# Weight conversions issued without a wait on the conversion before, in a layer of FFT attention and ternary feed-forward on eight cores

## The chip, the cores and the metric

The kernel runs on the 8 cores of one Trainium2 chip. Each core takes one of the 8 batch entries and computes it whole; the cores exchange nothing. The time is the device time of the slowest core, in microseconds (us).

## The reference

For each batch entry `x` is 2048 x 1024 (tokens x features), f32:

```python
xn = layernorm(x)                                 # over the 1024 features
q, k, v = xn @ Wq.T, xn @ Wk.T, xn @ Wv.T         # 1024 x 1024 each
mem = cumsum(fft(k) * fft(v), over the tokens)
attn = real(ifft(mem * conj(fft(q))))
h = silu(xn @ w1.T * w1_s) * (xn @ w2.T * w2_s)   # 4096 wide, weights -1, 0 or 1
h = gelu(h @ h1.T * h1_s)                         # 4096 x 4096
h = gelu(h @ h2.T * h2_s)                         # 4096 x 4096
return x + attn + h @ w3.T * w3_s
```

## The kernel before, in words

Activations lie with the features on the partitions and the tokens along the free dimension. Every f32 operand of a matrix product is split into a bf16 high part and a bf16 rest, and the products that matter are summed in PSUM; the ternary weights are exact in bf16.

There is no scheduler that reorders. `S.op(engine, emit, reads, writes, ...)` appends an operation to one list; each engine later executes its own operations in the order of that list. A tracker for each buffer holds the token of its last write and of the reads since. An operation waits for the last write of all that it reads, and for the last write and the reads of all that it writes. A DMA counts a semaphore up by 16 when it has landed; with `dma_sem` a name of its own is given to that semaphore. Loads are issued by SyncE (SP), stores to DRAM and the conversions below by GpSimd (POOL). A wait holds up everything behind it on its engine's list.

The stages:

1. Constants, the first layernorm (`emit_ln(0)`: x tile loaded to `XT`, sums by TensorE on L316 and L325, result `XNH` and `XNL`, stored to `xnh_scr` and `xnl_scr` by POOL on L368 and L371). Then Wq, Wk, Wv are multiplied with the Fourier matrices (L424) and written to DRAM as `wl_k`, `wl_v`, `wl_q`. A fence follows: every engine's next operation waits for all of this.
2. Conversion of the feed-forward weights from f32 to bf16, DRAM to DRAM, by DMAs on POOL's queue (L448 to L457): `w1c` to `w1b`, `w2c` to `w2b`, `h1c` to `h1b`, `h2c` to `h2b`, `w3c` to `w3b`. Each DMA reads 4 MB and writes 2 MB; there are 4 + 4 + 16 + 16 + 4 = 44. They write different parts of their tensor, but the tracker knows only the tensor as a whole, with one semaphore for each of the five.
3. Attention, 8 tiles of 256 tokens (`NT_A`, L459 on). In each: 24 projections (`proj`, L463: 8 each for k, v, q). One projection loads a slab `SLA` (L466, 512 KB, three buffers in turn; a slab's rows are runs of 512 bytes) on SP's queue, does 24 matmuls (L476) and a copy by ScalarE (L485). VectorE does the products and the scan over tokens. Then come the layernorm of the next tile (`emit_ln(t + 1)`) and the inverse transform: for each of 8 output chunks 32 matmuls (L570) into one of four PSUM banks, an add of x by VectorE into `ptc0` or `ptc1` in turn (L586), and a store to `part_scr` by POOL (L589). On POOL's list the 44 conversions stand first, then the `xnh_scr` and `xnl_scr` stores of tile 1, then the `part_scr` stores of tile 0, and so on.
4. A second fence, and the feed-forward: 4 tiles of 512 tokens (L593 on). L620 multiplies with w1 and w2, L657 with h1 and h2, L687 with w3; weights come from `w1b` to `w3b` by SP. The results go to `y`.

Of the kernel before, what the change touches and what calls it, by code (L numbers as in the profile page):

```python
# [58 lines left out]
class _Sched:  # L59
# [17 lines left out]
        return [(s, v, None, True) for s, v in self.counts.items() if v > 0]  # L77

    def op(self, eng, emit, reads=(), writes=(), extra_waits=(), dma=False,
           dma_sem=None):  # L80
        waits = {}
        def _add(tok):
            if tok is None:
                return
            sem, val, peng, pdma = tok
            if waits.get(sem, (0,))[0] < val:
                waits[sem] = (val,)
        for b in reads:
            _add(b.w)
        for b in writes:  # L90
            for t in b.rs:
                _add(t)
            _add(b.w)
        for t in extra_waits:
            _add(t)
        for t in self.fence_pending.pop(eng, ()):
            _add(t)
        if dma_sem is not None:
            sem = dma_sem
            amt = 16  # L100
            self.counts.setdefault(sem, 0)
        elif dma:
            i = self.rr[eng]
            self.rr[eng] = (i + 1) % self.NDMA
            sem = {"sync": "ds", "gpsimd": "dg", "scalar": "dc"}[eng] + str(i)
            amt = 16
            if self.counts[sem] > 0:
                _add((sem, self.counts[sem], None, True))
        else:
            sem = {"tensor": "tns", "vector": "vec", "scalar": "act"}[eng]  # L110
            amt = 1
        self.counts[sem] += amt
        tok = (sem, self.counts[sem], eng, dma)
        self.ops.append((eng, emit, [(s, v[0]) for s, v in waits.items()], sem, amt))
        for b in reads:
            b.rs.append(tok)
        for b in writes:
            b.w = tok
            b.rs = []
        return tok  # L120
# [22 lines left out]
def build_nc():  # L143
# [144 lines left out]
    def T(obj, tag=None):  # L288
        key = (id(obj), tag)
        if key not in trk:  # L290
            trk[key] = _Trk()
        return trk[key]
# [10 lines left out]
    for dst, src in ((s1c, s1m), (s2c, s2m), (sh1c, sh1m), (sh2c, sh2m), (s3c, s3m)):  # L303
        S.op("sync", lambda h, d=dst, s=src: h.dma_start(out=d[:], in_=s),
             writes=[T(dst)], dma=True)
# [97 lines left out]
    for w in "kvq":  # L403
        for kc in range(KC):
# [5 lines left out]
                writes=[T(wf32)], dma=True)  # L410
# [37 lines left out]
    for name, src, dst, nch, inner in (  # L448
            ("cw1", w1c, w1b, KC, NDIM * 512), ("cw2", w2c, w2b, KC, NDIM * 512),
            ("ch1", h1c, h1b, HC, HID * 128), ("ch2", h2c, h2b, HC, HID * 128),  # L450
            ("cw3", w3c, w3b, KC, HID * 128)):
        step = max(1, (4 << 20) // (inner * 4))
        for c0 in range(0, nch, step):
            c1 = min(nch, c0 + step)
            S.op("gpsimd",
                 lambda h, s=src, d=dst, a=c0, b=c1: h.dma_start(out=d[a:b], in_=s[a:b]),
                 writes=[T(dst)], dma=True, dma_sem=name)  # L457

    for t in range(NT_A):  # L459
        t0 = t * TA  # L460
# [103 lines left out]
        for dc in range(KC):  # L564
            bank = ps[dc % 4]
            def mm_inv_half(h, dc=dc, bank=bank, klo=0, khi=4, first=True, last=False):
                ins = None
                for la, lb in ((IM0, LH), (IM1, LH), (IM0, LL), (IML, LH)):
# [12 lines left out]
                 writes=[T(bank)])  # L581
            S.op("tensor", _ft.partial(mm_inv_half, klo=4, khi=8, first=False, last=True),
                 reads=[T(IM0), T(IM1), T(IML), T(LH, "hi"), T(LL, "hi")],
                 writes=[T(bank)])
# [179 lines left out]
```

How the kernel before makes its waits and increments, by code:

```python
            def run(h):  # L124
                watermark = {}
                for eng, emit, waits, sem, amt in self.ops:
                    if eng != eng_name:
                        continue
                    for sname, val in waits:
                        if watermark.get(sname, 0) < val:
                            h.wait_ge(sems[sname], val)
                            watermark[sname] = val
                    ins = emit(h)
                    ins.then_inc(sems[sem], amt)
# [579 lines left out]
        @block.sync  # L714
        def _(sync):
            for name, val in finals.items():
                if val > 0:
                    sync.wait_ge(sems[name], val)
```

## Time and profile before

| | us |
|---|---|
| runs shown, median of 2 | 8418.08 |
| runs shown, lowest and highest | 8376.08, 8460.08 |
| profiled execution, its own time | 7418.91 |
| profiled execution, span of the slowest core (core 5) | 7417.4 |
| profiled execution, spans of the eight cores | 7395.8 to 7417.4 |
| TensorE busy with matmuls in that span | 6159.7 (83%) |
| VectorE, ScalarE, GpSimd busy | 936.9, 521.1, 88.7 |
| mean granted TensorE clock, core 5 | 0.919 |

The profiled execution is about 1000 us shorter than the two timed runs. All times inside the kernel that are read below are positions in the span of the profiled execution, counted from its first instruction on core 5. "Landing" is the time from the issue of a DMA until its semaphore tells that it is complete. Engines are PE (TensorE), DVE (VectorE), ACT (ScalarE), POOL (GpSimd) and SP (SyncE); q1 is the DMA queue that SP's loads use and q0 the one that POOL's DMAs use; both run on the same 16 DMA engines of the core.

### The profile page before, as it was taken

How to read it: one execution, taken by the hardware profiler on the slowest of the kernel's cores; microseconds unless marked ns; L12 is line 12 of the kernel's file. 1: busy time of each engine (PE TensorE's matmuls, PEld its weight loads, DVE VectorE, ACT ScalarE, POOL GpSimd, SP SyncE). 2: the span in 40 equal slices, each digit the busy share in tenths (PEclk: the TensorE clock that was granted, in tenths of full speed). 3: DMA queues.
4: the chain of work that ended last, by engine and by line, in shares of the span. 5: the costliest groups of instructions: out<-in, count | busy, mean ns of one | idle time of the engine just before them, and what ended most of it. 6: DMA issues, size and time to landing. Idle time of an engine off the chain costs nothing.

```text
span 7417.4 us, 74350 instructions; the slowest of 8 cores (7395.8 to 7417.4 us)
## 1 busy us (share of the span) xinstructions
PE 6159.7 (83%) x31008; PEld 3047.0 (41%) x31008; DVE 936.9 (13%) x1519; ACT 521.1 (7%) x881; POOL 88.7 (1%) x160
## 2 busy tenths in 40 slices
PE   3873300288887999999989999999999999999999
PEld 1332100166655444444434444444444444444444
DVE  2110100032231210000120000011000002100000
ACT  2110000011110000000000000000000000000000
POOL 0000000000000000000000000000000000000000
PEclk6986655699988999999999999999999999999999
DMA  4129888743433233333323333332333332233333
GB/s 132 56 69 140 121 110 113 120 130 109 130 106 98 67 80 74 74 80 76 107 68 74 74 74 80 83 94 69 80 74 74 80 91 80 74 79 74 74 80 86
DMA packets 614490, 659.20 MB, mean 89 GB/s; under 512 B 14352, under 2 KB 587792, under 8 KB 611344
## 3 DMA queue, kind: packets, MB, share of 16 engines
q1 hardware_dynamic: 602704, 536.99, 28.8%
q0 software_dynamic: 11456, 117.45, 10.7%
q8 instruction: 252, 4.13, 0.2%
q14 instruction: 78, 0.64, 0.0%
HBM read 708.91 MB, written 130.02 MB: 113 GB/s over the span
## 4 chain that ended last, share of the span: by engine, by line
PE 77%; DMA 17%; DVE 3%; issue 2%; ACT 1%; SPq 0%; DVEq 0%; ACTq 0%; POOL 0%; POOLq 0%
PE ps L657 48%; PE ps L620 11%; PE ps L687 6%; PE ps L424 5%; DMA h1b<-h1c 4%; PE ps L476 4%; DMA h2b<-h2c 4%; PE ps L570 3%; DMA SLW<-w1b 2%; DMA w2b<-w2c 1%; DMA w3b<-w3c 1%; DMA w1b<-w1c 1%; PE ps L325 1%; DMA SLA<-wl_v 1%; DMA part_scr<-ptc 1%
## 5 line engine op out<-in xcount | busy, mean ns | idle before, releaser
L657 PE MATMUL ps<-GH,SLB 128*128 128x512 bf16 x4096 | 912.2, 381 | 18.9 <-DMA SLB<-h1b 18.9
L657 PE MATMUL ps<-H1H,SLB 128*128 128x512 bf16 x4096 | 911.7, 381 | 10.9 <-DVE H1L L669 10.9
L657 PE MATMUL ps<-GL,SLB 128*128 128x512 bf16 x4096 | 904.9, 379 | 0.0
L657 PE MATMUL ps<-H1L,SLB 128*128 128x512 bf16 x4096 | 904.9, 379 | 0.0
L657 PEld LDWEIGHTS ps<-GH,SLB 128*128 128x128 bf16 x4096 | 402.1, 98 | 508.7 <-issue 30.7
L657 PEld LDWEIGHTS ps<-H1H,SLB 128*128 128x128 bf16 x4096 | 402.0, 98 | 500.3 <-issue 22.0
L657 PEld LDWEIGHTS ps<-GL,SLB 128*128 128x128 bf16 x4096 | 400.9, 98 | 483.1
L657 PEld LDWEIGHTS ps<-H1L,SLB 128*128 128x128 bf16 x4096 | 400.8, 98 | 483.2
L570 PE MATMUL ps<-LH,IM0b 128*128 128x256 bf16 x512 | 82.0, 285 | 616.6 <-DVE ptc L586 595.3
L476 PE MATMUL ps<-XNH,SLA 128*128 128x256 bf16 x3072 | 399.4, 281 | 226.4 <-DMA SLA<-wl_q 85.8
L620 PE MATMUL ps<-XNFH,SLW 128*128 128x512 bf16 x2048 | 501.9, 389 | 96.3 <-DMA SLW<-w1b 68.8
L620 PE MATMUL ps<-XNFL,SLW 128*128 128x512 bf16 x2048 | 489.1, 382 | 0.0
L476 PEld LDWEIGHTS ps<-XNH,SLA 128*128 128x128 bf16 x3072 | 303.6, 101 | 289.5 <-issue 246.2
L620 PEld LDWEIGHTS ps<-XNFH,SLW 128*128 128x128 bf16 x2048 | 200.6, 99 | 357.0 <-issue 133.6
L424 PE MATMUL ps<-T,WHb 128*128 128x512 bf16 x768 | 186.5, 387 | 166.4 <-DVE WLb L413 166.4
L570 PEld LDWEIGHTS ps<-LH,IM0b 128*128 128x128 bf16 x512 | 46.3, 100 | 644.2 <-issue 638.6
L620 PEld LDWEIGHTS ps<-XNFL,SLW 128*128 128x128 bf16 x2048 | 202.7, 99 | 249.5 <-issue 14.4
L666 DVE CAST H1H<-tsil 128x512 bf16<-128x512 f32 x128 | 54.6, 427 | 1638.2 <-ACT tsil L663 1638.2
L666 DVE CAST GH<-tsil 128x512 bf16<-128x512 f32 x128 | 54.6, 427 | 1628.8 <-ACT tsil L663 1628.8
L687 PE MATMUL ps<-GH,SLB 128*128 128x512 bf16 x1024 | 227.9, 381 | 10.9 <-DVE GL L669 10.9
L687 PE MATMUL ps<-GL,SLB 128*128 128x512 bf16 x1024 | 226.2, 379 | 0.0
L476 PE MATMUL ps<-XNL,SLA 128*128 128x256 bf16 x1536 | 212.9, 285 | 0.0
(103 smaller groups left out, 2680.9 us busy)
## 6 DMA issues: line engine op xcount, KB each, us to landing
SLA<-wl_k SPq DMA_DIRECT2D x64, 512.0 KB, 5.5
SLA<-wl_v SPq DMA_DIRECT2D x64, 512.0 KB, 4.9
SLA<-wl_q SPq DMA_DIRECT2D x64, 512.0 KB, 4.5
h1b<-h1c POOLq DMA_DIRECT2D x16, 2048.0 KB, 18.9
h2b<-h2c POOLq DMA_DIRECT2D x16, 2048.0 KB, 18.3
SLW<-w1b SPq DMA_DIRECT2D x32, 1024.0 KB, 5.2
SLW<-w2b SPq DMA_DIRECT2D x32, 1024.0 KB, 5.3
XT<-x_ds SPq DMA_DIRECT2D x8, 1024.0 KB, 8.3
```

The lines of the kernel that those rows point to most:

```text
L325: S.op("tensor", lambda h, c=c, q=sqc: h.matmul(ps[5][0:1, 0:TA], ones_col[:], q[:], start=(c == 0), stop=(c == KC - 1)), reads=[T(sqc), T ...
L424: ins = h.matmul(bank[:], la[:, kc2, dc * 128:(dc + 1) * 128], lb[:, kc2, half * 512:half * 512 + 512], start=first, stop=(la is WH and lb ...
L476: ins = h.matmul(bank[:, 0:TA], sl[:, kc2, li, :], lb[:, kc2, :], start=(li == 0 and lb is XNH and kc2 == 0), stop=(li == 1 and kc2 == KC ...
L570: ins = h.matmul(bank[:, 0:TA], la[:, kc2, dc * 128:(dc + 1) * 128], lb[:, kc2, :], start=first, stop=(last and la is IML and kc2 == khi - 1))
L620: ins = h.matmul(bank[:, 0:TF], sl[:, kc2, ol * 128:(ol + 1) * 128], lb[:, kc2, :], start=first, stop=(lb is XL and kc2 == KC - 1))
L657: ins = h.matmul(bank[:, 0:TF], sl[:, kc2, :], lb[:, kc2, :], start=first, stop=(lb is inL and kc2 == HC - 1))
L666: S.op("vector", lambda h, oc=oc, oh=outH: h.tensor_copy(oh[:, oc, :], h32[:]), reads=[T(h32)], writes=[T(outH)])
L687: ins = h.matmul(bank[:, 0:TF], sl[:, kc2, :], lb[:, kc2, :], start=first, stop=(lb is H2L and kc2 == HC - 1))
```

## The change

`S.op` gets a flag `no_waw`. With it, an operation no longer waits for the last write of the buffers that it writes; waits for reads and for what it reads stay. The flag is set for the 44 conversions alone. Since each becomes its tensor's last write and counts the same semaphore up by 16, an operation that later reads the tensor waits, as before, for the count of all its conversions.

```diff
     def op(self, eng, emit, reads=(), writes=(), extra_waits=(), dma=False,
-           dma_sem=None):
+           dma_sem=None, no_waw=False):
@@
         for b in writes:
             for t in b.rs:
                 _add(t)
-            _add(b.w)
+            if not no_waw:
+                _add(b.w)
@@
             S.op("gpsimd",
                  lambda h, s=src, d=dst, a=c0, b=c1: h.dma_start(out=d[a:b], in_=s[a:b]),
-                 writes=[T(dst)], dma=True, dma_sem=name)
+                 writes=[T(dst)], dma=True, dma_sem=name, no_waw=True)
```

## Rows read from the trace of the kernel before

**Rows 1.** three stretches: engines busy (instructions), PEclk, DMA share, GB/s
```profile
900.00:1400.00 500.00, 0.00 (x0) 0.00 (x0) 0.00 (x0) 0.00 (x0) 13.44 (x27) 0.50 0.83 110
1448.00:2368.00 920.00, 762.38 (x6042) 587.12 (x6040) 256.23 (x409) 130.73 (x316) 42.77 (x71) 0.93 0.42 117
2368.00:7417.00 5049.00, 4909.45 (x22528) 2209.71 (x22528) 549.64 (x928) 274.21 (x392) 17.30 (x32) 0.99 0.33 79
```

**Rows 2.** who waited for whom: us in total, times, longest
```profile
PE ps L570 <- DVE ptc L586: 595.3, 1, 595.3
...
DVE ptc L586 <- DMA part_scr<-ptc: 726.0, 41, 604.0
...
POOL h1b L456 <- DMA h1b<-h1c: 329.1, 15, 42.5
```

**Rows 3.** timeline of POOL's conversion issues: start, duration, idle before
```profile
540.13 0.54 POOL L456 DMA_DIRECT2D w1b<-w1c  x1 [492.35 <-issue]
...
700.33 0.50 POOL L456 DMA_DIRECT2D w2b<-w2c  x1 [22.68 <-DMA w2b<-w2c]
...
743.81 0.50 POOL L456 DMA_DIRECT2D h1b<-h1c  x1 [42.50 <-DMA h1b<-h1c]
...
1037.36 0.50 POOL L456 DMA_DIRECT2D h1b<-h1c  x1 [19.04 <-DMA h1b<-h1c]
...
1075.25 0.50 POOL L456 DMA_DIRECT2D h2b<-h2c  x1 [36.91 <-DMA h2b<-h2c]
...
1339.62 0.50 POOL L456 DMA_DIRECT2D h2b<-h2c  x1 [18.98 <-DMA h2b<-h2c]
...
1377.34 0.50 POOL L456 DMA_DIRECT2D w3b<-w3c  x1 [36.73 <-DMA w3b<-w3c]
...
1415.06 0.50 POOL L456 DMA_DIRECT2D w3b<-w3c  x1 [18.37 <-DMA w3b<-w3c]
```

**Rows 4.** chain of waits, 1395 to 1450: start, us, what
```profile
1396.20 18.36 DMA w3b<-w3c
...
1417.40 19.58 DMA part_scr<-ptc
```

**Rows 5.** DMA issues of the whole run: KB each, median us to landing
```profile
part_scr<-ptc POOLq DMA_DIRECT2D x64, 128.0 KB, 2.4
```

**Rows 6.** DMA issues from 1037 to 1038 alone
```profile
h1b<-h1c POOLq DMA_DIRECT2D x1, 2048.0 KB, 22.5
h2b<-h2c POOLq DMA_DIRECT2D x1, 2048.0 KB, 36.9
```

**Rows 7.** DMA queues, 870 to 1330, conversions alone: packets, MB, share
```profile
q0 software_dynamic: 1936, 50.86, 82.8%
```

**Rows 8.** DMA queues, 545 to 555, one conversion under way
```profile
q0 software_dynamic: 46, 1.51, 125.8%
q1 hardware_dynamic: 46, 0.02, 1.1%
```

**Rows 9.** DMA queues, 608 to 612, between two conversions
```profile
q1 hardware_dynamic: 1594, 0.81, 94.9%
```

**Rows 10.** DMA queues, 540 to 544: packets, MB, share
```profile
q1 hardware_dynamic: 2066, 1.04, 93.3%
```

**Rows 11.** timeline of PE, 600 to 750: waits for slabs
```profile
653.65 1.87 PE L476 MATMUL ps<-XNH,SLA 128*128 128x256 bf16 x8 [28.70 <-DMA SLA<-wl_v]
...
745.21 1.86 PE L476 MATMUL ps<-XNH,SLA 128*128 128x256 bf16 x8 [32.86 <-DMA SLA<-wl_q]
```

**Rows 12.** timeline of PE, an undisturbed tile and the next one's start
```profile
1448.04 1.04 PE L476 MATMUL ps<-XNH,SLA 128*128 128x256 bf16 x8
...
1462.73 1.03 PE L476 MATMUL ps<-XNH,SLA 128*128 128x256 bf16 x8 [0.45 <-DMA SLA<-wl_k]
...
1577.88 1.04 PE L476 MATMUL ps<-XNH,SLA 128*128 128x256 bf16 x8
```

## The prediction, made before the changed kernel was run

> **What bounds the kernel now.** I read the stretches first. From 2368 to the end TensorE is busy for 4909 of 5049 us at a clock of 0.99, and the attention tiles from 1448 to 2368 keep it busy for 762 of 920; from 900 to 1400 it executes nothing at all, while the DMA engines are at 0.83 [rows 1]. The list of waits names the hole: PE waits once for 595.3 us, before the inverse transform of tile 0 (L570), for the vector add that frees a PSUM bank (L586), and that add waits for the store out of `ptc` [rows 2]. The store is no slow work. It stands on POOL's queue behind the 44 conversions of the weights (L456), and POOL waits before each of them until the one before has landed: 15 times in `h1b` alone. The reader is to see that the hole ends with the last conversion, not with anything that TensorE, VectorE or ScalarE does.
>
> The timeline of POOL gives their rhythm. The first is issued at 540.13 and the last at 1415.06 [rows 3]. Between 1075.25 and 1339.62 lie 14 steps, so 18.88 us for one transfer, of which 18.36 us is the way from issue to landing [rows 3, 4].
>
> **What the change takes away.** Each tensor's first conversion had no predecessor, so 44 - 5 = 39 waits go. The arithmetic, the bytes and the number of issues stay. POOL will issue all 44 back to back: 44 x 0.50 = 22 us, done at about 562, instead of 1415. Readers lose nothing: the last conversion of each tensor has counted the semaphore up only when all of them are in, and they start after 2368. So the question is what a queue that is full for the whole time changes, for itself, for what stands behind it and for what runs beside it.
>
> *Behind it.* The stores of tile 0 and the xn stores of tile 1 can now be issued before 1415, but they are on the same queue. The trace has the case: the first store out of `ptc` was issued at 1417.40, 2.3 us after the last conversion, and took 19.58 us to land where its median is 2.4 [rows 4, 5]. And of two conversions issued 0.49 us apart, the first landed after 22.5 and the second after 36.9 us: they go through one after the other, they don't share [rows 6]. So issuing the store early buys nothing; it lands when the conversions have drained.
>
> *For itself.* Before already has pairs of conversions without a wait between them, where one tensor ends and the next begins. From 1037.36 to 1075.25 two take 37.89 us, from 1339.62 to 1377.34 they take 37.72 [rows 3]: 18.9 us for one, against 18.88 one at a time. Taking the wait away gained nothing at either place. I take 18.88, so 44 x 18.88 = 831 us, and the last lands at 540 + 831 = 1371. The bounds: if all the idle share of the DMA engines between 870 and 1330 closed (they are at 82.8% there [rows 7]), 18.88 x 0.828 = 15.63 us, 688 us in all, last landing 1228. On the other side the pair from 700.33 to 743.81, which ran with slab loads beside it, took 43.48 us, 21.7 for one [rows 3]: 956 us, landing 1496. I stay by the middle, since that pair began with a burst of slab packets left over from the gap before it, and under one full queue there are no such bursts.
>
> The rows of the pairs can be held against a rule: in the Trainium skill, "DMA: Bandwidth & Descriptors", section "Anatomy of one DMA", each DMA of this kind carries about 2 us that do not depend on its size. By that rule 39 removed waits would hide up to 78 us, and the forecast would be 78 us lower. The pairs don't show it; it returns below as a rival worked out from rows.
>
> *Beside it: what I think decides.* During the conversions SP's queue brings the slabs `SLA` for the 24 projections of tile 0. From 545 to 555, with one conversion under way, the two queues put through 46 packets each: strictly one for one, but a conversion's packet is 33 KB (1.51 MB / 46) and a slab's 0.5 KB [rows 8]. Between two conversions the picture turns: from 608 to 612 the slab queue moves 1594 packets [rows 9]. A slab is 512 KB, about 1024 packets of 512 B (2066 packets were 1.04 MB [rows 10]). So tile 0 lives on the gaps that the waits make, and where a pair left no gap PE waited 28.7 and 32.9 us for its slabs [rows 11]. The change removes these gaps.
>
> How many slabs come in without them: two before the first conversion starts to move (2066 packets by 544 [rows 10]). A conversion has 80 packets (1936 packets for 50.86 MB, 2.1 MB each [rows 7]), so 44 of them are 3520, and one for one that is 3520 slab packets, 3.4 slabs. When the queue drains at 1371, 5.4 of 24 slabs are there and PE has done five projections; in before it had done all 24, the layernorm of tile 1 and most of the inverse transform of tile 0 before its wait of 595 us was over.
>
> What is left then costs what it costs in an undisturbed tile. Tile 1 begins at 1448.04, its sixth projection at 1462.73, and the next tile's first at 1577.88 [rows 12]: 115.2 us from the sixth on, with the layernorm, the inverse transform and its stores inside. Some 2 us go to the rest of the sixth slab (0.6 x 1024 packets at 1594 in 4 us [rows 9]). So tile 1 begins at 1371 + 2 + 115 = 1488, against 1448 in before: 40 us later.
>
> *The sum.* The conversions end 63 us earlier (1371 for 1415.06 + 18.9 = 1434), since no slab slows them; of tile 0, 117 us now come after them where 14 us did (1434 to 1448); 117 - 14 - 63 = +40. From there on nothing differs: the tiles and the hidden layers have the same queues and waits as before. The profiled execution's span is 7417.4 us and its time 7418.9; with the change 7459. The runs shown have a median of 8418.08, a thousand us above the profiled execution, and their two values lie 84 us apart; the trace can't say where that thousand is. I carry the 40 us over as they are: 8458. If all stretched alike (8418 / 7419 = 1.135) they would be 45.
>
> **Rivals.**
> - *The queue drains faster.* The engines idle 17% of the time between conversions, and a deep queue might fill this. Fully filled: 1228 + 117 = 1345, 103 us earlier than 1448, so 8315; half filled, 8387. For it speaks only the share; against it stand both clean pairs. Chance 0.18.
> - *The slabs get through.* If the engines don't keep to one for one under a long queue, tile 0 stays hidden, its bytes slow the conversions as before, and the time stays: 8418, or 20 us less for 39 gaps of 0.5 us between landing and next issue (18.88 - 18.36). The same holds if POOL can't in fact run ahead. Against it: the counts in [rows 8]. Chance 0.15.
> - *Slower by over 2%.* The interleaved small packets break the stream of large ones, and each conversion takes the 21.7 us of the pair at 700 throughout. Then 1496 + 117 = 1613, 165 us later: 8583. It passes 2% from 21.8 us a transfer on. For it speaks that pair; against it, that the burst at its start explains most of the excess. Chance 0.08.
> - *The stores pass the conversions.* If the `ptc` stores did not queue, PE would go on to tiles 1 and 2 during the conversions; even if slow slabs let only one and a half tiles of 130 us (1448.04 to 1577.88) be hidden, the time would fall by 195 us, to 8223. [Rows 4 to 6] speak against it. Chance 0.05.
>
> **How the numbers follow.** The forecast has 0.54, and its own range comes from the time of one transfer, a third of the way to either bound: 17.8 to 19.8 us, which is 48 us down and 41 us up, so 8410 to 8499. The whole range leaves out the last two rivals and the far end of the first: with 42 us for the spread of the two runs it is 8330 to 8545. A change under about 2%, 168 us, can't be told from none by this measurement. Over 2% faster: the passing stores, 0.05. Over 2% slower: the slow stream, 0.08. Within 2%: 0.87.
>
> **What would show it.** In the profile after, all 44 issues on POOL within 25 us of 540; projections of tile 0 (L476) two at 545 and then some three, about 240 us apart (831 / 3.4), until about 1371; in that stretch the two DMA queues with equal packet counts; the wait of PE no longer one of 595 us before L570 but several long ones for `SLA`; the layernorm of tile 1 (L316) only after 1400, and tile 1's first projection near 1488. The step on the queue is wrong if the last conversion lands before 1340 or after 1400; the step on the slabs is wrong if 24 projections are done by 900; the step on the stores is wrong if a `ptc` store lands before the last conversion. And all is wrong if the thousand us that the timed runs have over the profiled one lie in the conversions.

## The result

Before runs in 7413 to 7420 us and after in 7484 to 7501 us; the ratio is 1.0102, 95% interval 1.0086 to 1.0118: about 75 us slower, within the 2%. The two runs that stood ahead of the prediction, 8460 and 8376 us, belong to a slower kind of execution that occurs with either kernel (in one of 8455.89 us four cores show a TensorE clock of 0.79 and the other four 0.92), and every ratio here leaves that kind out.

The profiled executions stand at 7418.9 and 7488.0 us, 69 us apart. In this section core 5 is compared with core 5, since the rows of before are from it; the rows of the experiments are from the slowest core of each run. First the execution after in three stretches, columns as in [rows 1]:

```profile
600.00:700.00 100.00, 0.00 (x0) 0.00 (x0) 0.00 (x0) 0.00 (x0) 0.00 (x0) 0.50 0.99 111
900.00:1000.00 100.00, 0.00 (x0) 0.00 (x0) 0.00 (x0) 0.00 (x0) 0.00 (x0) 0.50 1.00 112
1400.00:1500.00 100.00, 78.88 (x595) 58.24 (x593) 35.47 (x56) 17.60 (x42) 2.38 (x3) 0.91 0.41 116
```

TensorE is idle where before it at least did the projections of tile 0, and the DMA engines are full, 0.99 and 1.00 where [rows 1] had 0.83. The hole has another owner now. The waits (us in total, times, longest):

```profile
PE ps L477 <- DMA SLA<-wl_k: 835.8, 12, 245.8
...
DVE ptc L587 <- DMA part_scr<-ptc: 122.8, 37, 7.4
```

The single wait of 595.3 us for `ptc` [rows 2] is gone, and the add waits 122.8 us for its stores in all instead of 726.0. In its place PE waits 835.8 us for k slabs. The timeline of POOL (start, duration, what, count):

```profile
546.51 2.06 POOL L457 DMA_DIRECT2D w1b<-w1c  x4 [496.13 <-issue]
548.53 2.02 POOL L457 DMA_DIRECT2D w2b<-w2c  x4
550.49 7.99 POOL L457 DMA_DIRECT2D h1b<-h1c  x16
558.32 8.08 POOL L457 DMA_DIRECT2D h2b<-h2c  x16
566.15 2.23 POOL L457 DMA_DIRECT2D w3b<-w3c  x4
1496.89 0.93 POOL L369 DMA_DIRECT2D xnh_scr<-XNH  x1 [928.50 <-DVE XNL L366]
```

The 44 conversions are issued within 22 us, as forecast, and POOL then waits 928.5 us for the layernorm of tile 1, which itself waits for slabs. The last conversion, issued at 567.6, lands 825 us later, at 1392.7 (DMA issues from 568.0 to 568.4: KB, us to landing):

```profile
w3b<-w3c POOLq DMA_DIRECT2D x1, 2048.0 KB, 825.1
```

The timeline of PE, the rows in which a slab was waited for, and the first matmuls of tile 1:

```profile
554.66 1.86 PE L477 MATMUL ps<-XNH,SLA 128*128 128x256 bf16 x8 [13.32 <-DMA SLA<-wl_k]
...
804.14 1.86 PE L477 MATMUL ps<-XNH,SLA 128*128 128x256 bf16 x8 [241.96 <-DMA SLA<-wl_k]
...
1052.24 1.86 PE L477 MATMUL ps<-XNH,SLA 128*128 128x256 bf16 x8 [243.36 <-DMA SLA<-wl_k]
...
1303.35 1.86 PE L477 MATMUL ps<-XNH,SLA 128*128 128x256 bf16 x8 [245.84 <-DMA SLA<-wl_k]
...
1394.20 1.86 PE L477 MATMUL ps<-XNH,SLA 128*128 128x256 bf16 x8 [86.52 <-DMA SLA<-wl_k]
...
1514.64 1.04 PE L477 MATMUL ps<-XNH,SLA 128*128 128x256 bf16 x8
```

Two projections, then one each 250 us, and the sixth only when the conversions are through: in 840 us PE gets three slabs. Tile 1 begins at 1514.64 for 1448.04 [rows 12]. Over the eight cores that start moved from a mean of 1443.5 to 1513.2, 69.7 us, on each core by 67 to 75; this is the whole difference of the two executions (69 us), so nothing is left for what comes behind it. The last conversion lands at 1429.1 in before and at 1389.7 in after, again as means over the cores: the queue is through 39 us earlier, and 123 us of tile 0 come after it where 14 came before. What the two DMA queues put through between 600 and 800 (packets, MB, share of the 16 engines' time):

```profile
q0 software_dynamic: 840, 22.02, 99.0%
q1 hardware_dynamic: 841, 0.43, 1.4%
```

841 slab packets beside 840 conversion packets, and 0.43 MB beside 22.02. (Of the 80 packets of a conversion 64 carry 32 KB each and 16 are of 4 bytes, so the mean is 26 KB.)

### The profile page after: what moved, and what is told of

Its sections match the earlier page's. It is cut to its first block, busy times and chain, and to the rows that moved or that the text cites. A ratio compares the mean times of both kernels' runs of the same rounds, so it can differ in the third digit from the quotient of the medians.

```text
span 7486.5 us, 74311 instructions; the slowest of 8 cores (7470.4 to 7486.5 us)
## 1 busy us (share of the span) xinstructions
PE 6151.5 (82%) x31008; PEld 3043.9 (41%) x31008; DVE 936.8 (13%) x1519; ACT 520.7 (7%) x881; POOL 88.6 (1%) x160
## 4 chain that ended last, share of the span: by engine, by line
PE 77%; another core or an unknown queue 11%; DMA 5%; DVE 4%; issue 1%; ACT 1%; SPq 0%; DVEq 0%; ACTq 0%; POOLq 0%; POOL 0%
PE ps L658 47%; PE ps L621 11%; PE ps L688 6%; PE ps L477 5%; PE ps L425 5%; PE ps L571 3%; DMA SLW<-w1b 2%; PE ps L326 1%; DMA SLA<-wl_v 1%; DMA part_scr<-ptc 1%; DMA SLB<-h1b 0%; DVE WLb L414 0%; DMA SLA<-wl_k 0%; ACT WHb L412 0%
## 5 line engine op out<-in xcount | busy, mean ns | idle before, releaser
L664 ACT ACTIVATE tsil<-ps,sh2c 128x512 f32<-128x512 f32 x128 | 87.9, 687 | 1698.4 <-PE ps L658 1698.4
L664 ACT ACTIVATE tsil<-ps,sh1c 128x512 f32<-128x512 f32 x128 | 88.0, 687 | 1622.6 <-PE ps L658 1622.5
```

Of the source, the lines that this page charges most:

```text
L664: S.op("scalar", lambda h, oc=oc, bank=bank, sc=sc_col: h.activation(h32[:], bank[:, 0:TF], AF.Gelu, scale=sc[:, oc:oc + 1]), reads=[T(ban ...
```

## The experiments

Two theories. **Theory 1:** the two queues take turns packet by packet, so while a conversion is under way the slabs get next to nothing; before, the waits on POOL opened gaps in which they came in; after has no gaps, and the part of tile 0 that was hidden behind the conversions comes after them. **Theory 2:** the long queue is itself slower than one transfer at a time, and the time is lost there.

**Waits gone only where no slab is needed.** The first 18 conversions keep their waits, the last 26 are issued at once:

```diff
-                 writes=[T(dst)], dma=True, dma_sem=name, no_waw=True)
+                 writes=[T(dst)], dma=True, dma_sem=name,
+                 no_waw=(name in ("ch2", "cw3") or (name == "ch1" and c0 >= 20)))
```

> The waits stay on the first 18 conversions (w1, w2 and ten of h1), until all slabs of tile 0 are in; the last 26 conversions are issued at once. Theory 1 (removing the waits costs only because tile 0's slabs starve): tile 0 runs as before, all 24 projections done by about 800, and the long queue has nothing beside it; each of the 26 takes the 18.9 us of before, tile 1 begins within 5 us of before, ratio to before 0.999 to 1.001. Theory 2 (a long queue is by itself slower, 19.2 us a conversion against 18.9): 26 x 0.3 = 8 us later, ratio 1.001, and the trace shows 19.2 us a conversion with no slab beside it.

Its profiled execution took 7432.65 us and its fastest 7426.74, beside 7413.64 for the fastest of before. There is no ratio with an interval for it; fastest against fastest is 1.0018, an indication only, and just above both expectations. PE waits (same columns):

```profile
PE ps L572 <- DVE ptc L588: 587.0, 1, 587.0
```

This is the picture of before again, one wait of 587 us for `ptc`. Seven of the eight cores begin tile 1 between 1439 and 1448, as before; core 0, which issued its first conversion 15 us late, begins it at 1452.9, and it is the slowest. The time of one conversion, counted by packets over 440 us and all cores (80 packets each), is 18.95 us, against 18.87 in before. That leaves theory 2 some 0.1 us a transfer, 3.5 us over 44; it is not what costs 70.

This run also shows what a store does behind a full queue. POOL is through with its 44 issues at 945 and then issues the first store out of `ptc` and, when that has landed, the second (timeline of POOL, core 0):

```profile
946.45 0.56 POOL L591 DMA_DIRECT2D part_scr<-ptc  x1
1443.61 0.56 POOL L591 DMA_DIRECT2D part_scr<-ptc  x1 [496.59 <-DMA part_scr<-ptc]
```

The store was issued about 460 us earlier than in before (1405 on core 0) and took 496.6 us to land, 3 us after the last conversion (1440.2). Issuing it early bought nothing, as the prediction says.

**Waits gone only among w1 and w2.** `no_waw=name in ("cw1", "cw2")`.

> Only the waits among the 8 conversions of w1 and w2 are gone; h1, h2 and w3 keep theirs. Theory 1: the slabs starve for 8 x 19 = 154 us, PE waits about that long after its second projection, and then tile 0 is made up in the gaps of h1, ending near 960 instead of 840; that is still well before the conversions end, so nothing is lost: ratio 0.999 to 1.001. The rival, that every starved stretch costs in proportion to its waits (6 of 39), gives +11 us, ratio 1.0015.

Ratio 0.9984, interval 0.994 to 1.0027, which by itself excludes neither case (the rival's is 1.0015). But tile 1 begins at 1441.2 as a mean over the cores, 1443.5 in before, where the rival wants it 11 us later. The waits of PE, slowest core:

```profile
PE ps L571 <- DVE ptc L587: 453.0, 1, 453.0
...
PE ps L477 <- DMA SLA<-wl_k: 195.8, 6, 164.0
```

The slabs did starve, for 164 us at a stretch, and the wait for `ptc` became shorter for it: 453 us for 595. A starved stretch costs nothing as long as it ends early enough for tile 0 to fit in behind it. The cost is not a sum over the waits removed.

**Slabs held back altogether.** As after, but the first slab load of tile 0 waits for all conversions:

```diff
+                hold = ([T(b).w for b in (w1b, w2b, h1b, h2b, w3b)]
+                        if t == 0 and wname == "k" and rc == 0 else [])
...
-                    reads=[T(wl_scr[wname])], writes=[T(sl)], dma=True)
+                    reads=[T(wl_scr[wname])], writes=[T(sl)], dma=True,
+                    extra_waits=hold)
```

> As after, but the first slab load of tile 0 waits until all conversions have landed, so the conversions have the DMA engines to themselves. Theory 1 with a trickle that costs nothing: conversions end when they do in after (1391 on core 5), then a whole tile of 131 us and 4 us of start: tile 1 begins at 1526, 12 us after that of after; ratio to before 1.012. If the one-for-one slab packets are what makes a conversion 19.2 us instead of 18.9, they end 13 us earlier, near 1378, and the ratio is 1.010. Either way it costs what after costs within 15 us, which says that after gets almost nothing done in the 850 us.

Ratio 1.0083, interval 1.0035 to 1.0131. Holding all slabs back for the whole time costs about the same as what after does: tile 1 begins at 1517.6 for 1513.2 (means over the cores). The two queues from 600 to 1200 on the slowest core, here and then in after on its slowest core:

```profile
q0 software_dynamic: 2556, 66.98, 100.2%
```

```profile
q0 software_dynamic: 2504, 65.57, 98.3%
q1 hardware_dynamic: 2504, 1.27, 1.3%
```

With the slabs away 2556 conversion packets pass in 600 us, with them 2504. From 600 to 1360 and over all cores that is 18.91 us a conversion alone and 19.17 beside slabs. So the price of the trickle is 0.26 us a conversion, 11 us in all, and the queue alone runs at the pace of before. The expectation's second branch came (conversions end 15 us sooner than in after, 1374.5 for 1389.7; ratio 1.010 expected, within the interval).

**Slab packets of 4 KB.** `wl_k`, `wl_v`, `wl_q` are laid out so that each partition of a slab is one run of 4 KB; everything else as in after.

```diff
-    wl_scr = {w: scr(f"wl_{w}", [KC, 2, 128, 1024], BF16) for w in "qkv"}
+    wl_scr = {w: scr(f"wl_{w}", [KC, 128, KC, 256], BF16) for w in "qkv"}
...
-                    out=d[:],
-                    in_=s[:, rc // 4, :, (rc % 4) * 256:(rc % 4) * 256 + 256]
-                        .rearrange("c p (l m) -> p c l m", l=2)),
+                    out=d[:].rearrange("p c l m -> p (c l m)"),
+                    in_=s[rc].rearrange("p c x -> p (c x)")),
```

> As after (no waits), but the slabs lie in DRAM so that one packet is 4 KB instead of 512 B: 128 packets a slab instead of 1024. Theory 1 (the two queues go one for one by packets, whatever their size): 3520 conversion packets let 27 slabs through; projections come about every 31 us, the 24th near 1250; the x tile of tile 1 (1024 packets) is what is late, it lands with the end of the conversions, and tile 1 begins 55 to 60 us after their end, near 1450, as in before: ratio 0.998 to 1.002. If the sharing goes by bytes or the cost comes from the long queue itself, it stays at 1.010.

Ratio 1.0003, interval 0.9964 to 1.0041. The queues from 600 to 1200 and the waits, slowest core:

```profile
q0 software_dynamic: 2415, 63.41, 93.6%
q1 hardware_dynamic: 2415, 8.78, 6.3%
```

```profile
PE ps L477 <- DMA SLA<-wl_v: 261.4, 17, 35.1
...
PE ps L317 <- DMA XT<-x_ds: 99.4, 3, 85.3
```

Again one for one, 2415 and 2415, but now that is 8.78 MB of slabs for 1.27: the longest wait for a slab falls from 247 to 35 us, and tile 0's projections all come in during the conversions. What was late is what was expected to be, the x tile of tile 1 with its packets of 1 KB (85.3 us). Tile 1 begins at 1476 on this core, not at the 1450 I had written: a conversion beside so many more slab bytes takes 19.8 us, so the last one lands at 1422, and the 54 us behind it are the 55 to 60 expected.

**The control: slab packets of 4 KB with the waits kept.**

> As before (waits kept), with slab packets of 4 KB alone: the control for the run with 4 KB slabs and no waits. Tile 0 is hidden here anyway; what can change is the 44 us that the later tiles wait for slabs, of which perhaps half goes, and a few us of the conversions that share with slabs: ratio to before 0.995 to 0.999. If 4 KB slabs and no waits then lies above this by less than 0.002, removing the waits no longer costs anything.

Ratio 0.9963, interval 0.9948 to 0.9978. Larger slab packets are worth 0.4% by themselves, so without the waits there is still a difference of 0.0040 between this pair of kernels, where it is 0.0102 between the original pair. I had put the bound at 0.002. By the ratios three fifths of the cost went with the packet size; the intervals are as wide as what is left, but the traces bear it out. The last conversion lands at the same time with and without the waits (1420.4 and 1419.2, means over the cores), so slower conversions are not what remains. Tile 1 begins 15 us after it with the waits (1435.0) and 54 us after it without (1473.1), and those 38 us are where the x tile is late.

**Conversion packets of 4 KB.** The other side of the same balance: slabs as in after, a conversion cut into rows of 2048 elements.

```diff
-                 lambda h, s=src, d=dst, a=c0, b=c1: h.dma_start(out=d[a:b], in_=s[a:b]),
+                 lambda h, s=src, d=dst, a=c0, b=c1: h.dma_start(
+                     out=d[a:b].rearrange("c (r s) m -> r c (s m)", s=2048 // d.shape[2]),
+                     in_=s[a:b].rearrange("c (r s) m -> r c (s m)", s=2048 // s.shape[2])),
```

> As after (no waits), slabs of 512 B as before, but each conversion is cut into rows of 2048 elements, so that a packet writes 4 KB instead of 32 KB: 8 times as many packets. Theory 1: one for one lets 28000 slab packets through, 27 slabs, and tile 0 is hidden as with the 4 KB slabs; if the conversions keep 19 to 20 us each, tile 1 begins near 1450 to 1490 and the ratio is 1.000 to 1.006. If small packets make the conversions slow (25 us each), they end 250 us later and the ratio is 1.03. If the size of the packets doesn't matter: 1.010.

Ratio 1.0063, interval 1.0034 to 1.0093. The queues from 600 to 1200, slowest core:

```profile
q0 software_dynamic: 15832, 62.88, 91.0%
q1 hardware_dynamic: 15823, 7.97, 8.5%
```

15832 against 15823: one for one at 4 KB against 0.5 KB too, and 7.97 MB of slabs come in. The slabs' longest wait is 37 us. The ratio is at the upper edge of what was expected, as is the time of a conversion with its slabs, 20 us (62.88 MB in 600 us); tile 1 begins at 1486.6, 53 us after the last landing (means over the cores). Another limit shows here: POOL issues its last four conversions only at 1038, where after is done at 568, behind an idle stretch of 321 us in which it waits for no semaphore that the profile shows. The reading that fits is that with 528 packets in a conversion instead of 80 its queue took no more for so long; then taking a wait out of the program does not always let POOL run ahead of the transfers.

**Only the stores on another queue.** The stores to `xnh_scr`, `xnl_scr` and `part_scr` are issued by ScalarE (`S.op("scalar", ...)` for `S.op("gpsimd", ...)`); first without the waits, then with them:

> As after (no waits, slabs and conversions in their old packets), only the stores of the attention tiles go to ScalarE's queue. Theory 1 says that in after it is the slabs that hold tile 0, long before any store: PE still does one projection each 245 us, tile 1 begins as late as in after, ratio to before 1.008 to 1.011. If it were the stores behind the conversions that cost the time, this would be faster than before.

> As before (waits kept, old packets), the stores of the attention tiles on ScalarE's queue. PE no longer waits 595 us for a store; it goes on with tiles 1 and 2 by the slabs that come in the gaps between conversions, three a gap, some 230 to 260 us a tile. Until the conversions end (about 1530, since each shares with slabs) 2.5 to 3 tiles are hidden: ratio 0.965 to 0.98. Beside the run without waits this says what the gaps are worth: 0.03 or more with these stores, 0.01 without. If the gaps carry fewer than three slabs: 0.985.

Without the waits 1.0077 (1.0048 to 1.0107), with them 0.9793 (0.9713 to 0.9873). The same edit does nothing clear of the noise for after, whose own ratio is 1.0102 (tile 1 begins at 1511.9 for 1513.2, the longest wait for a slab is 246.8 us), and gives before 2%. This pair shows both halves of the mechanism: in after the slabs hold PE and no store is near; in before PE has its slabs and the store is what stops it. And it prices the waits and the gaps that they make: 0.028 of the time, 210 us, as soon as PE can use what comes through them.

**Packet sizes and stores together.** Three kernels with 4 KB slabs and the stores on ScalarE's queue: conversions of 4 KB and no waits, conversions of 1 KB and no waits, conversions of 4 KB with the waits of before.

> No waits, 4 KB packets in slabs and conversions, and the stores of the attention tiles (xn and part) issued by ScalarE on its own queue instead of POOL's, so that they don't stand behind the conversions. Theory 1 (what held the tiles was first the slabs' share, then the stores behind the conversions): with 4 KB against 4 KB up to 220 slabs get through, the tiles run beside the conversions, which end near 1600 because of the shared bytes, and the attention ends 450 to 700 us earlier than 2367: ratio 0.91 to 0.94. If a store waits in the DMA engines also on another queue, or the slabs stay slow: ratio 0.98 to 1.0.

> No waits, stores on ScalarE's queue, slabs in packets of 4 KB, conversions in packets of 1 KB (rows of 512 elements). One for one now gives slabs four times a conversion's bytes, so the tiles run nearly undisturbed, 140 to 180 us each, and the conversions take what is left and end between 1650 and 1800: ratio 0.94 to 0.965. If packets of 1 KB make the conversions themselves slow (over 25 us each alone), they end after 1800 and the feed-forward waits for them: ratio 0.97 to 1.0.

> Waits kept, stores on ScalarE's queue, slabs and conversions both in packets of 4 KB: the run without waits of this kind was at 0.9795. If the waits matter only because they open gaps for starved slabs, they are worth little once slabs get through inside a conversion: within 0.005 of the run without waits, 0.975 to 0.985. If the gaps still help (x tiles and stores have packets of 1 KB and 512 B), it is faster: 0.965 to 0.975.

Ratios 0.9795 (0.9753 to 0.9837), 0.9659 (0.9631 to 0.9687) and 0.9603 (0.9537 to 0.9668). How much TensorE does from 550 to 1400, columns as in [rows 1], in this order: before, after, before with the stores moved, and these three.

```profile
550.00:1400.00 850.00, 121.20 (x779) 84.44 (x776) 35.50 (x56) 19.94 (x48) 20.92 (x42) 0.57 0.87 120
```

```profile
550.00:1400.00 850.00, 26.98 (x141) 18.66 (x142) 0.00 (x0) 1.86 (x5) 17.13 (x35) 0.51 0.99 113
```

```profile
550.00:1400.00 850.00, 327.33 (x2133) 235.54 (x2134) 76.68 (x126) 45.82 (x112) 18.43 (x37) 0.68 0.96 140
```

```profile
550.00:1400.00 850.00, 356.67 (x2000) 237.97 (x2000) 76.11 (x124) 43.96 (x107) 33.76 (x39) 0.66 1.00 139
```

```profile
550.00:1400.00 850.00, 442.56 (x2820) 312.70 (x2820) 114.17 (x186) 63.04 (x153) 75.56 (x38) 0.74 1.01 147
```

```profile
550.00:1400.00 850.00, 471.90 (x3108) 336.06 (x3108) 128.04 (x203) 67.81 (x166) 29.90 (x34) 0.76 0.92 154
```

779 matmuls in before, 141 in after, 3108 in the best: the work of the attention tiles moves in beside the conversions, and the clock rises from 0.51 to 0.76 with it. My first estimate for the no-waits form, 0.91 to 0.94, was far off: I took 4 KB against 4 KB for enough. What fits is that x tiles (1 KB) and stores (1 KB and 512 B) take their turns too: a `part_scr` store lands there after 12.5 us (median from 600 to 1400), where before has 2.4. The run with 1 KB conversions came out just above its expectation, and the same may hold for it (10.7 us a store); against 4 KB it gains 0.014. Of the two with 4 KB conversions, the one without waits waits 176.8 us for `ptc` and 125.2 us for x tiles; with the waits kept the first is 81.0 and the second 45.3 (us in total, times, longest; slowest core):

```profile
PE ps L573 <- DVE ptc L589: 176.8, 4, 82.9
...
PE ps L317 <- DMA XT<-x_ds: 125.2, 4, 39.4
```

```profile
PE ps L572 <- DVE ptc L588: 81.0, 8, 29.1
...
PE ps L316 <- DMA XT<-x_ds: 45.3, 5, 15.1
```

So the waits help even here, by 0.019, against my expectation of 0.005. That the small packets use the gaps is the reading that fits these rows; it is not shown, since no run separates it from a conversion's own packets. One more kernel has the stores on ScalarE and 4 KB slabs with old conversions and waits. Its expectation:

> Waits kept, conversions in 32 KB packets as before, slabs of 4 KB, stores of the attention tiles on ScalarE's queue. The slabs go by the gaps that the waits make (three slabs a gap) and one for one inside a conversion: about 100 to 130 slabs, 4 to 5 tiles, during the conversions, which stretch to 22 to 24 us each. The attention ends 300 to 400 us earlier: ratio 0.945 to 0.96. If the gaps are too short for three slabs: 2 tiles, ratio 0.975.

It has one run that can be compared, 7230.60 us beside a median of 7423.10 for before: 0.974, an indication only. That is the lesser gain of the two cases expected, and close to the 0.9793 with the old slabs.

The version that beats both kernels by most keeps the waits: 4 KB packets in slabs and conversions, stores off POOL's queue, a ratio of 0.9603, and 7137.67 us in its profiled execution for 7418.91 of before.

## Why the prediction was right or wrong

**The base of the sum failed.** I carried +40 us over to the median of the two runs then shown, 8458 us, with a range of 8330 to 8545; the kernel takes 7484 to 7501 and before takes 7413 to 7420, just what its profiled execution took. The step that failed is the one in which I took the 1000 us above the profiled execution as part of both kernels. The profiled execution's own time plus the change, 7459, which stood in the text beside it, would have been off by 29. A base worked out from the profiled execution, with the timed median as a second case, would have left the size of the change as the only error.

The lower bound of the range, 8330, follows from no term of the text either: the half-filled queue less the spread is 8387 - 42 = 8345.

**The direction and the class held.** Slower within 2%, forecast 1.005, measured 1.010. The cause is the one forecast, so this is not luck.

**The size was half.** The step that failed here is *For itself*, which took 18.88 us for a conversion as if the slab packets beside it were free, with smaller parts from two other terms. Tile 1 was to begin 40 us later and began 69.7 us later, as a mean over the cores:
- *Time of a conversion, 18.88 us.* From the first issue to the last landing pass 846 us (543.6 to 1389.7), 19.23 for each of the 44, where I had 831. In the middle of the stretch it is 19.17 beside the slab packets and 18.91 without them. The pairs of [rows 3] gave the pace of the queue alone correctly; that slab packets have a price I had seen in my upper bound and put at nothing. 15 us.
- *Start, 540.1.* Core 5 was the earliest but one of before; the mean over the cores is 543.9 in before and 543.6 in after. A sum anchored on the means gives +48 for +40: 8 us.
- *What is left of tile 0, 117 us.* It is 123.5, and 121.9 on core 5. There the sixth to the last projection take 64.5 us (1394.2 to 1458.7) where the undisturbed tile of [rows 12] took 60.6. Part of it is that the first matmuls after the idle stretch run at the lower of the two clock levels (1.86 us for eight at 1394.20, with a granted clock of 0.56 from 1390 to 1400; 1.03 for eight at 1462.73 in [rows 12]). 6 to 7 us.

Together 30 us, which is what lies between +40 and +69.7.

**The mechanism was right as written.** Two projections first, 3.4 slabs beside 3520 packets (three more projections before the conversions ended, 250 us apart for the 244 forecast), the sixth at the end, packet counts equal, POOL done within 22 us, wait for `ptc` gone. That an early store is no shorter way out is shown twice: behind the 26 free conversions it took 496.6 us to land, and moving the stores to another queue in after gained nothing. [Rows 6] with their order of landing were read rightly. One reading was rough: a conversion's packet is not 33 KB throughout, but 32 KB for 64 of the 80 and 4 bytes for the rest; the count of 80, on which the 3.4 slabs rest, is right.

**The rivals.** The queue that drains faster did not show: with all waits gone and nothing beside it a conversion takes 18.91 us for 18.87. The rule of the Trainium skill that I had set beside the pairs, about 2 us that don't depend on size ("DMA: Bandwidth & Descriptors", "Anatomy of one DMA"), would by estimate have made it some 17 us (18.88 - 2); the measurement decides against it for these transfers with all eight cores at it. The slow stream (21.7 us) was the wrong size but the right sign: 19.2 to 20.0 beside slabs. The slabs did not get through. In after itself no store was there to pass, since the first was issued only after the last conversion; where one was, it did not pass (946.45 above). On the sharing, the same page of the Trainium skill says in "Queues, rings and completion order" that a DMA engine goes round its queues at packet granularity. The counts 840 and 841 agree with that, if the packets that the profile counts are those; the page gives a packet some 9 to 17 descriptors, and no run here shows how many one of the counted packets holds.

## What to carry to other kernels

When two queues share the DMA engines, look at the packet sizes of both before the bytes: here each queue got the same number of packets, so a load of small packets beside a stream of large ones almost stood still, and a wait that looks like waste in the issuing queue may be what lets the load through. Before a wait is removed, ask what runs in the gap that it makes. And a cost that was hidden shows up only when the cover ends: here starving tile 0 for 164 us cost nothing, for 840 us 1%.

## What the runs showed of the hardware

A full queue of DRAM-to-DRAM conversions brought the busy share of the DMA engines from 0.83 to 1.00 and the pace from 18.87 to 18.91 us for 4 MB read and 2 MB written: the idle sixth between single transfers was worth nothing. What closed the gaps was that each packet took longer, 3.76 us on average (1.002 x 16 x 600 / 2556, the run with the slabs held back) for 3.15 (0.828 x 16 x 460 / 1936, [rows 7]); what sets the pace then, no run shows. The busy share was no measure of what could be won.

While both queues had work all the time, they took turns packet by packet to within one packet in 800, at each pairing of sizes tried: 32 KB with 0.5 KB (840 and 841 in 200 us), 32 KB with 4 KB (2415 and 2415 in 600 us), 4 KB with 0.5 KB (15832 and 15823).

Within one queue the order of issue was kept: a store of 128 KB issued behind the 26 conversions without waits landed when they were through, after 496.6 us, where the median is 2.4; on ScalarE's queue, beside queued conversions of 4 KB packets, the median was 12.5.
